# Seven half-block products for gate and up in the last group of a ternary gated FFN

## The chip, the cores and the metric

One core of a Trainium2 chip runs one program. The time is the device time of a run in microseconds. A core has TensorE (PE, matrix products into PSUM), VectorE (DVE), ScalarE (ACT), GpSimd (POOL) and SyncE (SP, which here issues nearly all DMAs). Each engine works through its own instructions in order; semaphores tie them together. PSUM has eight banks of 128 x 512 single-precision numbers.

## The reference

Input x is 2 x 1024 x 512 in single precision. Cut to what matters:

```
x = x + gated_delta(layernorm(x), Wq, Wk, Wv, Wo, Wb, bb, Wd, bd)   # a linear attention with a scan over time
n = layernorm(x)                          # [2, 1024, 512]
quantize(w) = clip(round(w / (mean|w| + 1e-8)), -1, 1)
gate = n @ quantize(w1).T                 # w1, w2: [1408, 512]
up   = n @ quantize(w2).T
x = x + (sigmoid(gate) * up) @ quantize(w3).T       # w3: [512, 1408]
```

The weights become -1, 0 and 1, which half precision holds exactly. An activation is split into a high half-precision part and the rest, a low one; both are multiplied, and PSUM adds them.

## The kernel before, in words

The 1024 time steps are 8 chunks of 128 for each of the 2 batch rows. Attention goes chunk by chunk. The FFN goes by groups of two chunks (`G = 4` groups, 512 tokens each). While group g is in the FFN, the attention and second normalisation of chunks 2g+2 and 2g+3 are worked in between its units; group 3 has no such work.

A group has `UNITS = 15` units (`group`, L1186 on TensorE). Units 0 to 10 are the 11 blocks of 128 hidden rows: 8 matmuls of 512 columns for gate, 8 for up (4 blocks of the contraction, high and low part, L1199), into three PSUM banks in turn (`bank_free`, L1174). ScalarE takes the sigmoid of gate (L718) and then the high part of the hidden block (L724), VectorE multiplies up with the sigmoid (L989, one operand in PSUM) and subtracts for the low part (L994). Units 11 to 14 are the down products of the four token blocks, 22 matmuls each (L1217); the last of the whole kernel is made in two halves of 256 columns. VectorE adds each to the residual (L1005) and SP stores it.

The order is written out by hand. Tables `PE_AFTER`, `DVE_AFTER`, `ACT_AFTER`, `POOL_AFTER` (L238 on) say behind which unit of group g the steps of the two next chunks stand on each engine: `chain`, `levels`, `masks`, `o`, `state`, `oT`, `wo`, `resid`, `norm2`, `apply`, `xhi`, `xlo`. The last ones prepare the next group's tokens. `norm2` gives mean and variance (VectorE) and the scale (six small GpSimd instructions, L402 to L408); `apply` (L915) writes the normalised, scaled values; `xhi` (L651, ScalarE) makes the high part, `xlo` the low one, for batch row 0 on GpSimd (L480) and for row 1 on VectorE (L921). SP then issues two DMA transposes of 128 x 1024 (L319, `turn_x`), which lay the tokens along the free dimension. For the second chunk these stand at units 11 and 12, beside the down products. TensorE waits for all transposes of a group at its start:

```
pe.wait_ge(xT_in, 64 * g + 64)
```

PSUM holds three banks `ffn` for the FFN; `lev`, `oc` (two banks each) and `pd` are the attention's, unused in group 3.

Of the kernel before, what the change touches and what calls it, by code (L numbers as in the profile page):

```python
# [16 lines left out]
def build_gated_delta_ternary_ffn(nc, x, Wq, Wk, Wv, Wo, Wb, bb, Wd, bd, w1, w2, w3, out):  # L17
# [5 lines left out]
    P = 128  # L23
# [11 lines left out]
    XS = 2048.0  # L35
# [3 lines left out]
    assert B == 2 and 2 * K == P and V == P and DT == 4 and XS * D ** 0.5 < 65504 and HS * D < 65504  # L39
# [7 lines left out]
    with ctx:  # L47
# [14 lines left out]
        wqk = sb("wqk", [P, DT, 2 * K])  # L62
        wbd = sb("wbd", [P, DT, 2 * K])
        wv = sb("wv", [P, DT, V])
# [7 lines left out]
        xn = sb("xn", [P, 2, B, D])  # L72
        xn2 = sb("xn2", [P, B, D])
# [28 lines left out]
        xT = w_nat[:, WN:WN + G * XT].bitcast(f16).rearrange("p (g s t n) -> p g s t n", g=G, s=2, t=DT)  # L102
        abs_out = [w12T[:, DT * k:DT * k + DT, 2 * P:2 * P + SL // DT] for k in range(2)]
        late = xnT[:, :, :, :, :].rearrange("p a t b n -> p (a t b n)")
        sig = late[:, 0:2 * 512].rearrange("p (s n) -> p s n", s=2)
        hid32 = late[:, 2 * 512:4 * 512].rearrange("p (s n) -> p s n", s=2)
# [9 lines left out]
        xT_last = w_nat[:, WN + (G - 1) * XT:WN + G * XT]  # L116
        scratch_front = [Scratch(w3T_flat[:, 8 * P * n:8 * P * (n + 1)]) for n in range(2)]
        scratch_late = [Scratch(xT_last[:, 8 * P * n:8 * P * (n + 1)]) for n in range(2)]
# [44 lines left out]
                                                    sem("lo_ready"))  # L163
        down_done, y_ready, y_stored = sem("down_done"), sem("y_ready"), sem("y_stored")
# [77 lines left out]
        POOL_AFTER = {"fetch": (0, 3), "norm2": (6, 11), "xlo": (7, 12)}  # L242

# [16 lines left out]

        def xT_tile(c, b):

            at = 2 * (c % 2) + b
            return xT[:, c // 2, :, :, at * P:(at + 1) * P].rearrange("p s t n -> p (s t) n")
# [14 lines left out]
        def _(sp_):  # L279
# [35 lines left out]
            def turn_x(c):  # L315

                for b in range(B):
# [37 lines left out]
            for g in range(G):  # L355
                for u in range(UNITS):
# [5 lines left out]
                    if g < G - 1:  # L362
                        for s, k in stages(DVE_AFTER, u):
                            if s == "xlo":
                                turn_x(2 * g + 2 + k)
# [5 lines left out]
        def _(pool):  # L371
# [92 lines left out]
            def norm2(c):  # L464
                pool.wait_ge(stats2_ready, c + 1)
                rstd(c, C + c, mv2, rs2, XS).then_inc(rstd2_ready, 1)

            def attn(s, c):
                if s == "fetch":
                    fetch(c)  # L470
                if s == "norm2":
                    norm2(c)
                if s == "xlo":
                    xlo(c)

            def xlo(c):
                if c > 1:
                    pool.wait_ge(xT_in, 16 * B * (c - 1))
                pool.wait_ge(xhi_ready, B * c + 1)
                nc.gpsimd.tensor_tensor(halves(c)[:, 0, 1, :], xn2[:, 0, :], halves(c)[:, 0, 0, :],  # L480
                                        ALU.subtract).then_inc(xlo0_ready, 1)

# [17 lines left out]
            for u in range(UNITS):  # L500
                for s, k in stages(POOL_AFTER, u):
                    if (s, k) != ("fetch", 0):
                        attn(s, 2 + k)
# [7 lines left out]
            for g in range(1, G - 1):  # L511
# [5 lines left out]
                norm2(2 * g + 2)  # L517
                xlo(2 * g + 2)
                norm2(2 * g + 3)
                xlo(2 * g + 3)  # L520
                if g == 1:
                    gates(7)

        @block.scalar
        def _(act):
# [105 lines left out]
            def attn(s, c):  # L631
# [624 lines left out]
```

## Time and profile before

| | us |
|---|---|
| runs, median (lowest to highest) | 328.49 (328.21 to 328.55) |
| profiled execution, first to last instruction (span) | 327.1 |
| TensorE busy | 319.8 (98%) |
| VectorE busy | 210.1 (64%) |
| ScalarE busy | 142.4 (44%) |
| GpSimd busy | 107.4 (33%) |
| L1199, gate and up: 704 matmuls | 155.4 |
| L1217, down: 374 matmuls | 76.7 |

The page gives the profiled execution's span and no other time of it; the runs' times are taken around the program and hold a little more. Busy is the time in which an engine had at least one instruction under way. A matmul's own duration (379 ns for 512 columns) is longer than the distance to the next, since they are pipelined; sums are made with the distance. "Idle before, releaser" names what ended the idle time in front of an instruction.

### The profile page before, as it was taken

Reading aid. Unit: us, or ns where it says so; the run is one execution under the profiler, and the core shown is the slowest. Engines: PE = TensorE matmul, PEld = TensorE weight load, DVE = VectorE, ACT = ScalarE, POOL = GpSimd, SP = SyncE. Lnnn points to the kernel's source line nnn. Section 1 sums busy time; section 2 is a strip of 40 time slices with the busy share of each in tenths; the row PEclk is TensorE's granted clock in tenths of the full one; section 3 lists DMA queues with packets and bytes.
Section 4 is the critical chain, followed back from the end, with each engine's and each line's share of the span. In section 5 each row is a group of like instructions: output and inputs, shape, how many; then the busy total and the mean of one; then the engine's idle time right before and its main releaser. Section 6 shows DMA issues by size and latency. Waiting matters only on the chain.

```text
span 327.1 us, 5876 instructions
## 1 busy us (share of the span) xinstructions
PE 319.8 (98%) x2152; PEld 176.1 (54%) x2152; DVE 210.1 (64%) x474; ACT 142.4 (44%) x281; POOL 107.4 (33%) x339
## 2 busy tenths in 40 slices
PE   7999999999999999999999999999999999999996
PEld 5888779874445444445454444454544444444445
DVE  6789899899998767366688543666886312433311
ACT  3687896789855571323143260231431102232200
POOL 7298325599913016980030136500201100000000
PEclk9999999999999999999999999999999999999999
DMA  6999900647841625300003051000030720000011
GB/s 180 382 388 395 360 4 0 104 91 133 125 85 32 114 49 81 113 0 2 0 2 64 2 129 61 7 2 0 2 64 0 93 102 1 0 2 0 0 66 64
DMA packets 45805, 26.99 MB, mean 83 GB/s; under 512 B 37584, under 2 KB 38352, under 8 KB 45776
## 3 DMA queue, kind: packets, MB, share of 16 engines
q1 hardware_dynamic: 45456, 26.62, 31.0%
q8 instruction: 17, 0.28, 0.4%
q14 instruction: 12, 0.10, 0.1%
q10 hardware_dynamic: 320, 0.00, 0.0%
HBM read 13.89 MB, written 4.19 MB: 55 GB/s over the span
## 4 chain that ended last, share of the span: by engine, by line
PE 78%; DVE 10%; DMA 3%; SPq 3%; ACT 2%; issue 2%; DVEq 0%; ACTq 0%
PE ffn L1199 40%; PE ffn L1217 23%; PE lev L1120 4%; DMA x_sb<-in_L_attn_x_dram 3%; PE ffn L1044 3%; DVE w_nat L841 2%; DVE X L854 2%; SPq L282 2%; PE lev L1077 2%; PE pd L1054 2%; PE oc L1104 1%; DVE abs_part L821 1%; DVE w_nat L848 1%; DVE xnT L989 1%; DVE sc L881 1%
## 5 line engine op out<-in xcount | busy, mean ns | idle before, releaser
L1199 PE MATMUL ffn<-w_nat,w12T 128*128 128x512 f16 x704 | 155.4, 379 | 0.6 <-DVE xnT L989 0.6
L1199 PEld LDWEIGHTS ffn<-w_nat,w12T 128*128 128x128 f16 x704 | 67.8, 98 | 83.0 <-issue 3.7
L1217 PE MATMUL ffn<-w3T,w_nat 128*128 128x512 f16 (+1 forms) x374 | 76.7, 366 | 0.0
L718 ACT ACTIVATE xnT<-ffn 128x512 f32<-128x512 f32 x44 | 26.1, 593 | 97.5 <-PE ffn L1199 97.5
L989 DVE SCALAR_TENSOR_TENSOR xnT<-ffn,xnT 128x512 f32<-128x512 f32 x44 | 30.2, 687 | 52.3 <-PE ffn L1199 51.9
L1217 PEld LDWEIGHTS ffn<-w3T,w_nat 128*128 128x128 f16 x374 | 36.6, 98 | 40.7 <-ACT w_nat L724 1.0
L402 POOL TENSOR_TENSOR ve<-mv,rconst 128x2 f32<-128x2 f32 x12 | 2.5, 210 | 118.1 <-DVE mv L758 118.1
L1005 DVE SCALAR_TENSOR_TENSOR x_sb<-ffn,x_sb 128x512 f32<-128x512 f32 (+1 forms) x17 | 11.2, 659 | 42.8 <-PE ffn L1217 42.8
L994 DVE TENSOR_TENSOR w_nat<-xnT,w_nat 128x512 f16<-128x512 f32 x44 | 32.2, 732 | 0.4
L724 ACT ACTIVATE w_nat<-xnT 128x512 f16<-128x512 f32 x44 | 27.4, 623 | 8.4 <-DVE xnT L989 8.3
L881 DVE COPY_PREDICATED sc<-mask,lev 128x128 f32<-128x128 uint32 x56 | 18.9, 338 | 2.9 <-PE oc L1091 1.3
L854 DVE TENSOR_TENSOR X<-X,tmk 128x256 f32<-128x256 f32 x42 | 19.1, 454 | 1.4
L754 DVE BATCH_NORM_STATS2 stats<-x_sb 128x6 f32<-128x512 f32 x26 | 16.7, 683 | 0.4
L1044 PE MATMUL ffn<-xnT,wqk 128*128 128x256 f32 x64 | 15.7, 389 | 1.2 <-ACT xnT L542 0.8
L1054 PE MATMUL pd<-wv,xnT 128*128 128x128 f32 x128 | 15.8, 275 | 0.0
L1054 PEld LDWEIGHTS pd<-wv,xnT 128*128 128x128 f32 x128 | 15.2, 192 | 0.6 <-issue 0.5
L613 ACT ACTIVATE q<-w_nat,unround 128x512 f16<-128x512 f32 x22 | 14.3, 711 | 2.4 <-DVE w_nat L841 1.6
L1044 PE MATMUL ffn<-xnT,wbd 128*128 128x256 f32 x64 | 15.1, 379 | 0.0
L1120 PE MATMUL lev<-wo,oT 128*128 128x512 f32 x28 | 13.3, 598 | 0.6 <-DVE S L896 0.5
L1044 PEld LDWEIGHTS ffn<-xnT,wqk 128*128 128x128 f32 x64 | 11.5, 190 | 3.4 <-issue 1.0
L1044 PEld LDWEIGHTS ffn<-xnT,wbd 128*128 128x128 f32 x64 | 12.2, 190 | 1.7
L440 POOL TENSOR_TENSOR tot<-tot 128x32 f32<-128x32 f32 (+5 forms) x48 | 12.4, 258 | 0.0
(142 smaller groups left out, 368.2 us busy)
## 6 DMA issues: line engine op xcount, KB each, us to landing
x_sb<-in_L_attn_x_dram SPq DMA_DIRECT2D x16, 256.0 KB, 8.4
out_dram<-x_sb SPq DMA_DIRECT2D x15, 256.0 KB, 2.0
w_nat<-in_L_ffn_w_dram SPq DMA_DIRECT2D x2, 1536.0 KB, 12.2
w_nat<-in_L_ffn_w_dram SPq DMA_DIRECT2D x2, 1408.0 KB, 14.7
w_nat<-in_L_ffn_w_dram SPq DMA_DIRECT2D x2, 1280.0 KB, 12.9
wv<-in_L_attn_Wv_dram SPq DMA_DIRECT2D x1, 256.0 KB, 5.8
wo<-in_L_attn_Wo_dram SPq DMA_DIRECT2D x1, 256.0 KB, 13.5
out_dram<-x_sb SPq DMA_DIRECT2D x2, 128.0 KB, 1.7
```

The source lines that it names most:

```text
L718: nc.scalar.activation(sig[:, u % 2, :], bank[2 * u % 3][:, :], ACT.Sigmoid, scale=1.0 / XS).then_inc(sig_ready, 1)
L724: nc.scalar.activation(hid[:, 0, u - 1, :], hid32[:, (u - 1) % 2, :], ACT.Copy).then_inc(hi_ready, 1)
L754: done = nc.vector.bn_stats(stats[:, c, b, :], tile(c, b))
L854: step = nc.vector.tensor_tensor(FG(c, l + 1).rearrange("p (n h) -> p n h", h=h), FG(c, l).rearrange("p (n h) -> p n h", h=h), factors(c, ...
L881: link(nc.vector.copy_predicated(sc[:, :, :].rearrange("p b (n two h) -> p b n two h", two=2, h=h)[:, :, :, 1, :], level(mask[:, l, :], l) ...
L989: nc.vector.scalar_tensor_tensor(hid32[:, u % 2, :], bank[(2 * u + 1) % 3][:, :], HS / XS, sig[:, u % 2, :], ALU.mult, ALU.mult).then_inc( ...
L994: nc.vector.tensor_tensor(hid[:, 1, u - 1, :], hid32[:, (u - 1) % 2, :], hid[:, 0, u - 1, :], ALU.subtract).then_inc(lo_ready, 1)
L1044: done = nc.tensor.matmul(z_bank(c)[:, a * 256:(a + 1) * 256], w[:, t, :], turned(c)[:, t, :, :], start=t == 0, stop=t == DT - 1)
L1054: done = nc.tensor.matmul(pd[:, b * V:(b + 1) * V], turned(c)[:, t, b, :], wv[:, t, :], start=t == 0, stop=t == DT - 1)
L1120: done = nc.tensor.matmul(wo_bank(c, b)[:, :], oT[:, b, :], wo[:, :], start=True, stop=True)
L1199: done = nc.tensor.matmul(bank[n % 3][:, :], w12T[:, a * DT + t, u * P:(u + 1) * P], xT[:, g, part, t, :], start=t == 0 and part == 0, sto ...
L1217: done = nc.tensor.matmul(bank[(2 * HT + m + h) % 3][:, cols], hid[:, part, j, m * P:(m + 1) * P], w3T[:, j, cols], start=part == 0 and j ...
```

## The change

Group 3 (`FAST`) computes gate and up differently; groups 0 to 2 keep their products. The normalised tokens of group 3 are seen as a 2 x 2 block matrix: A11, A12 are the first and second 256 features of batch row 0 (`xn2(0)`), A21, A22 those of row 1. The weights are a 2 x 2 block matrix too, gate and up, each with its first and second 256 features. The product of two 2 x 2 block matrices takes eight block products; here it takes seven, of sums of blocks, which are added up in shared sums (products 1 to 7 below). Each block product of a unit is 128 hidden rows by 256 tokens with a contraction of 256.

- Weight sums `T1` to `T4` (128 x 2 x 1408 in half precision) are made on VectorE in group 2, behind units 2, 3, 4 and 11 (`T_AT`); T1 overwrites a block of up that is no longer needed.
- Token sums `xsum` (four, 128 x 256 each) are made on GpSimd for chunks 6 and 7. The plain blocks (3 of 256) and the sums (4 of 256) are split in high and low parts and turned by two DMA transposes a chunk, of 1536 and 2048 columns. The scale of the tokens is 512 in place of 2048.
- Four banks serve: unit u has a bank for products 1, 6, 7, 4 (`bank_a`) and one for 2, then 5, 3 (`bank_c`). ScalarE copies product 1 into `bank_c` as the seed on which product 2 adds, and keeps copies of the sums after product 6 and 7; VectorE adds them to `bank_c` for up; the multiplication with the sigmoid moves from VectorE to GpSimd, in two halves.
- Units k and k-1 are interleaved on TensorE. Product 1 of unit 0 stands four matmuls before the end of group 2. The last unit's products 4 and 3 stand among the first down matmuls.
- Moved: for chunk 7 SP's transposes stand at unit 13 in place of 12, behind the store of the second down tile, and `xlo` on VectorE at 13. The sums' splits: high on ScalarE at units 8 and 13, low on GpSimd.
- Tables for a group that follows another fast one are in the code too; with `FAST = (3,)` they are not used. `w_proj`, `x_all`, `xT(g)` and `scratch_late` lay memory out anew.

The products, in the order of one unit; the code writes A21, A22 as `A11(1)`, `A12(1)`:

| product | bank | weights | tokens | TensorE waits for |
|---|---|---|---|---|
| 1 | a | gate_w[0] | A11 | sigmoid_b of unit u-2 |
| 6 | a | T2 | A21 + A22 - A11 | seed |
| 2 | c (on the seed) | gate_w[1] | A12 | nothing more |
| 7 | a | T3 | A11 - A21 | keep_u2 |
| 5 | c | T1 | A21 + A22 | sigmoid_a |
| 4 | a | T4 | A22 | keep_u3 |
| 3 | c | up_w[1] | A12 - (A21 + A22 - A11) | up_b |

```diff
-    XS = 2048.0
+    XS, XS_FAST = 2048.0, 512.0
+    FAST = (3,)
+    HP = 2 * P
...
+        T1 = w12T[:, DT:DT + 2, :]
+        gate_w = [w12T[:, 2 * n:2 * n + 2, :] for n in range(2)]
+        up_w = [w12T[:, DT + 2 * n:DT + 2 * n + 2, :] for n in range(2)]
...
+        DVE_NEXT_FAST = DVE_AFTER | {"xlo": (8, 13)}
+        ACT_NEXT_FAST = {"gt": (2, 7), "oT": (4, 9), "xhiN": (7, 12), "xhiS": (8, 13)}
+        SP_NEXT_FAST = {"turn": (9, 13)}
...
+        T_AT = {2: (3,), 3: (2,), 4: (4,), HT: (1,)}
...
+        def bank_a(u):
+            return (bank[2], pd)[u % 2]
+        def bank_c(u):
+            return bank[u % 2]
...
+                if is_fast(c):            # SP, turn_x
+                    sp_.wait_ge(xlo1_ready, c + 1)
+                    sp_.dma_start_transpose(xT_N..., flat_N[c % 2]).then_inc(xT_in, 16)
+                    sp_.wait_ge(xlo0_ready, c + 1)
+                    sp_.dma_start_transpose(xT_S..., flat_S[c % 2]).then_inc(xT_in, 16)
...
+                if is_fast(c):            # GpSimd, xlo
+                    pool.wait_ge(xhi_ready, B * c + 2)
+                    for n in range(4):
+                        done = nc.gpsimd.tensor_tensor(split_S[c % 2][:, n, 1, :], xsum[:, n, :],
+                                                       split_S[c % 2][:, n, 0, :], ALU.subtract)
+                    done.then_inc(xlo0_ready, 1)
...
+                nc.gpsimd.tensor_tensor(xsum[:, 2, :], A11(0), A11(1), ALU.subtract)      # sums0
+                link(nc.gpsimd.tensor_tensor(xsum[:, 0, :], A11(1), A12(1), ALU.add))
+                link(nc.gpsimd.tensor_tensor(xsum[:, 1, :], xsum[:, 0, :], A11(0), ALU.subtract))   # sums1
+                nc.gpsimd.tensor_tensor(xsum[:, 3, :], A12(0), xsum[:, 1, :], ALU.subtract).then_inc(sums_ready, 1)
...
+            for g in FAST:                # GpSimd
+                for k in range(HT + 2):
+                    if k > 1:
+                        hidden_a(g, k - 2)
+                    if 1 <= k <= HT:
+                        hidden_b(g, k - 1)
...
+            def fast_group(g):            # ScalarE
+                for k in range(HT + 1):
+                    if k > 0:
+                        keep_u3(g, k - 1)
+                    if k < HT:
+                        seed(g, k)
+                    if k > 1:
+                        hidden_hi(g, k - 2)
+                    if k < HT:
+                        keep_u2(g, k)
+                    if k > 0:
+                        sigmoid_b(g, k - 1)
+                    if k < HT:
+                        sigmoid_a(g, k)
+                hidden_hi(g, HT - 1)
...
+                if n == 3:                # VectorE, weight_sum
+                    done = nc.vector.tensor_tensor(T3, up_w[1], up_w[0], ALU.subtract)
+                if n == 2:
+                    done = nc.vector.tensor_tensor(T2, T3, gate_w[0], ALU.add)
+                if n == 4:
+                    done = nc.vector.tensor_tensor(T4, gate_w[1], T2, ALU.subtract)
+                if n == 1:
+                    done = nc.vector.tensor_tensor(T1, up_w[0], gate_w[0], ALU.subtract)
...
+            def fast_group(g):            # VectorE
+                for k in range(HT + 1):
+                    if k > 0:
+                        up_b(g, k - 1)
+                    if k > 1:
+                        hidden_lo(g, k - 2)
+                    if k > 0:
+                        up_a(g, k - 1)
+                hidden_lo(g, HT - 1)
...
+                            if m == DT - 1 and n == 2 * HT - 4 and g + 1 in FAST:   # TensorE, group 2
+                                pe.wait_ge(xT_in, 64 * g + 128)
+                                product1(g + 1, 0)
...
+            def product(out, weights, u, tokens, first):
+                for t in range(2):
+                    for part in range(2):
+                        done = nc.tensor.matmul(out[:, 0:HP], weights[:, t, u * P:(u + 1) * P], tokens[:, part, t, :],
+                                                start=first and t == 0 and part == 0, stop=t == 1 and part == 1, skip_group_check=not first)
+                return done
...
+            def fast_group(g):            # TensorE
+                pe.wait_ge(T_ready, 4)
+                for k in range(HT):
+                    if k > 0:
+                        product1(g, k)
+                        product5(g, k - 1)
+                        product4(g, k - 1)
+                    product6(g, k)
+                    product2(g, k)
+                    if k > 0:
+                        product3(g, k - 1)
+                    product7(g, k)
+                pe.wait_ge(sig_b_ready, fast_n(g, HT - 1))
+                pe.wait_ge(hi_ready, g * HT + 6)
+                product5(g, HT - 1)
+                for n in range(2):
+                    down(g, 0, n, LATE_LAST)
+                product4(g, HT - 1)
+                for n in range(2, 6):
+                    down(g, 0, n, LATE_LAST)
+                product3(g, HT - 1)
+                for n in range(6, 2 * HT):
+                    part, j = LATE_LAST[n]
+                    pe.wait_ge((hi_ready, lo_ready)[part], g * HT + j + 1)
+                    down(g, 0, n, LATE_LAST)
...
```

## Rows read from the trace of the kernel before

**Rows 1.** The page, busy time of the engines and the granted clock in 40 slices
```profile
PE 319.8 (98%) x2152; PEld 176.1 (54%) x2152; DVE 210.1 (64%) x474; ACT 142.4 (44%) x281; POOL 107.4 (33%) x339
...
PEclk9999999999999999999999999999999999999999
```

**Rows 2.** Window of gate and up in group 3: length, busy us by engine, granted clock, DMA share
```profile
267.40:305.40 38.00, 38.00 (x178) 17.21 (x176) 12.98 (x20) 11.75 (x21) 0.00 (x0) 1.00 0.02 8
```

**Rows 3.** The chain that ended last, its last pieces: start, us, what
```profile
267.44 37.99 PE ffn L1199 x176
305.43 19.06 PE ffn L1217 x110
```

**Rows 4.** Timeline, end of the last down tile: start, us, engine, line, op [idle before <-releaser]
```profile
322.11 0.42 DVE L1005 SCALAR_TENSOR_TENSOR x_sb<-ffn,x_sb 128x256 f32<-128x256 f32 x1 [1.71 <-PE ffn L1217]
324.51 0.42 DVE L1005 SCALAR_TENSOR_TENSOR x_sb<-ffn,x_sb 128x256 f32<-128x256 f32 x1 [1.98 <-PE ffn L1217]
324.20 0.27 PE L1217 MATMUL ffn<-w3T,w_nat 128*128 128x256 f16 x1
```

**Rows 5.** Groups by line and shape from 190 us: count, then busy us and mean ns of one
```profile
L1199 PEld LDWEIGHTS ffn<-w_nat,w12T 128*128 128x128 f16 x352 | 34.1, 98 | 41.4 <-issue 0.9
...
L724 ACT ACTIVATE w_nat<-xnT 128x512 f16<-128x512 f32 x22 | 13.7, 623 | 4.2 <-DVE xnT L989 4.2
L718 ACT ACTIVATE xnT<-ffn 128x512 f32<-128x512 f32 x22 | 13.1, 597 | 67.9 <-PE ffn L1199 67.9
...
L480 POOL TENSOR_TENSOR xn<-xn 128x512 f16<-128x512 f32 x2 | 2.3, 1152 | 2.9 <-ACT xn L651 2.9
...
L639 ACT ACTIVATE oT<-oc 128x256 f32<-128x256 f32 x2 | 0.8, 384 | 2.1 <-PE lev L1109 1.8 <-PE oc L1104 0.3
...
L424 POOL TENSOR_TENSOR w_nat<-w_nat 128x128 f32<-128x128 f32 x1 | 0.5, 456 | 6.2 <-DVE w_nat L813 6.2
```

**Rows 6.** Timeline in group 0, a matmul that waited for VectorE
```profile
89.18 0.67 DVE L989 SCALAR_TENSOR_TENSOR xnT<-ffn,xnT 128x512 f32<-128x512 f32 x1
...
90.00 1.24 PE L1199 MATMUL ffn<-w_nat,w12T 128*128 128x512 f16 x5 [0.55 <-DVE xnT L989]
```

**Rows 7.** Timeline of VectorE, units 2 to 5 of group 2
```profile
217.38 0.69 DVE L989 SCALAR_TENSOR_TENSOR xnT<-ffn,xnT 128x512 f32<-128x512 f32 x1 [0.47 <-PE ffn L1199]
...
220.84 0.69 DVE L989 SCALAR_TENSOR_TENSOR xnT<-ffn,xnT 128x512 f32<-128x512 f32 x1 [2.17 <-PE ffn L1199]
...
225.58 0.69 DVE L989 SCALAR_TENSOR_TENSOR xnT<-ffn,xnT 128x512 f32<-128x512 f32 x1 [2.84 <-PE ffn L1199]
```

**Rows 8.** Timeline, chunk 7 from its statistics to its transposes
```profile
253.23 0.69 DVE L1005 SCALAR_TENSOR_TENSOR x_sb<-ffn,x_sb 128x512 f32<-128x512 f32 x1 [1.58 <-PE ffn L1217]
...
253.60 0.20 POOL L408 TENSOR_TENSOR rs<-rs 128x2 f32<-128x2 f32 x1
253.84 0.99 DVE L915 TENSOR_SCALAR xn<-x_sb,mv,rs 128x512 f32<-128x512 f32 x2
...
254.47 1.15 ACT L651 ACTIVATE xn<-xn 128x512 f16<-128x512 f32 x2 [6.35 <-DVE xn L915]
255.24 1.15 POOL L480 TENSOR_TENSOR xn<-xn 128x512 f16<-128x512 f32 x1 [1.45 <-ACT xn L651]
255.72 1.22 DVE L921 TENSOR_TENSOR xn<-xn 128x512 f16<-128x512 f32 x1 [0.89 <-ACT xn L651]
256.42 2.62 SPq L319 DMA_TRANSPOSE w_nat<-xn  x2
257.98 0.69 DVE L1005 SCALAR_TENSOR_TENSOR x_sb<-ffn,x_sb 128x512 f32<-128x512 f32 x1 [1.04 <-PE ffn L1217]
```

**Rows 9.** DMA issues in 237 to 238 and in 256 to 257 us: count, median us to landing
```profile
w_nat<-xs SPq DMA_TRANSPOSE x1, 3.0
...
w_nat<-xn SPq DMA_TRANSPOSE x1, 5.0
```

**Rows 10.** Timeline of VectorE, the low halves of chunk 6
```profile
240.94 0.68 DVE L921 TENSOR_TENSOR xs<-xn,xs 128x512 f16<-128x512 f32 x1
```

More of the change, by code:

```diff
@@ L510, in _ @@
             gates(4)
-            for g in range(1, G - 1):
+            for g in range(1, FAST[0]):
                 fetch(2 * g + 2)
@@ L739, in _ @@
             for g in range(G):
-                group(g)
+                if g in FAST:
+                    fast_group(g)
+                else:
+                    group(g)
         @block.vector
@@ L871, in attn @@
                     chain(c, range(4, NL))
-                if s == "masks":
+                if s == "chainA":
+                    dve.wait_ge(factors_ready, c + 1)
+                    dve.wait_ge(stored, c + 1)
+                    dve.wait_ge(o_done, c)
+                    chain(c, (0,))
+                if s == "chainB":
+                    chain(c, (1, 2))
+                if s == "chainC":
+                    chain(c, (3,))
+                if s == "chainD":
+                    chain(c, (4, 5))
+                if s == "chainE":
+                    chain(c, (6,))
+                if s == "norm2a":
+                    dve.wait_ge(resid_ready, c + 1)
+                    carry_wait()
+                    nc.vector.bn_stats(stats2[:, c, 0, :], tile(c, 0))
+                if s == "norm2b":
+                    link(nc.vector.bn_stats(stats2[:, c, 1, :], tile(c, 1)))
+                    carry_wait()
+                    for b in range(B):
+                        done = nc.vector.bn_aggr(mv2[:, c, b, :], stats2[:, c, b, :])
+                    done.then_inc(stats2_ready, 1)
+                if s == "sums":
+                    dve.wait_ge(xn2_ready, B * c + 2)
+                    dve.wait_ge(xhi_ready, B * c)
+                    nc.vector.tensor_tensor(xsum[:, 2, :], A11(0), A11(1), ALU.subtract)
+                    link(nc.vector.tensor_tensor(xsum[:, 0, :], A11(1), A12(1), ALU.add))
+                    link(nc.vector.tensor_tensor(xsum[:, 1, :], xsum[:, 0, :], A11(0), ALU.subtract))
+                    nc.vector.tensor_tensor(xsum[:, 3, :], A12(0), xsum[:, 1, :], ALU.subtract).then_inc(sums_ready, 1)
+                if s == "xloS":
+                    dve.wait_ge(xhi_ready, B * c + 2)
+                    nc.vector.tensor_tensor(split_S[c % 2][:, :, 1, :], xsum[:, :, :], split_S[c % 2][:, :, 0, :],
+                                            ALU.subtract).then_inc(xlo0_ready, 1)
+                if s in ("masks", "masks0", "masks1", "masks2", "masks3"):
                     dve.wait_ge(levels_done, c + 1)
@@ L1222, in group @@
-                    if g < G - 1:
-                        for s, k in stages(PE_AFTER, u):
-                            attn(s, 2 * g + 2 + k)
+                        for n in range(2 * HT):
+                            if m == 0:
+                                pe.wait_ge((hi_ready, lo_ready)[n // HT], g * HT + n % HT + 1)
+                                if g == 0 and n < HT:
+                                    pe.wait_ge(w3_in[n % QS], 16 * (n // QS + 1))
+                            if m == DT - 1 and n == 2 * HT - 4 and g + 1 in FAST:
+                                pe.wait_ge(xT_in, 64 * g + 128)
+                                product1(g + 1, 0)
+                            down(g, m, n, PARTS_IN_TURN)
@@ L1225, in group, with down @@
+                    for s, c in PE_AT.get((g, u), ()):
+                        attn(s, c)
                     if g == 0 and u == 0:
                         spread(1)
+            PARTS_IN_TURN = [(part, j) for part in range(2) for j in range(HT)]
+            LATE_LAST = ([(part, j) for part in range(2) for j in range(HT - 3)]
+                         + [(part, j) for j in range(HT - 3, HT) for part in range(2)])
+            def down(g, m, n, order):
+                part, j = order[n]
+                done = nc.tensor.matmul(down_bank(g, m)[:, :], hid_at(g, part, j, m), w3T[:, j, :], start=n == 0,
+                                        stop=n == 2 * HT - 1)
+                if n == 2 * HT - 1:
+                    done.then_inc(down_done, 1)
@@ new lines, in down_last @@
+            def down_last(g, m):
+                for h in range(2):
+                    cols = slice(h * D // 2, (h + 1) * D // 2)
+                    for n, (part, j) in enumerate(PARTS_IN_TURN):
+                        done = nc.tensor.matmul(down_bank(g, m + h)[:, cols], hid_at(g, part, j, m), w3T[:, j, cols],
+                                                start=n == 0, stop=n == 2 * HT - 1)
+                    done.then_inc(down_done, 1)
+            def product(out, weights, u, tokens, first):
[4 more added lines that the diff above has]
+                return done
```

376 lines of the change are left out of this document (309 added, 67 removed).

## The prediction

> **What bounds the kernel now.** I read the page's first parts, then the windows by stage, then the chain of waits, then single instructions. TensorE is busy 319.8 of 327.1 us, and the granted clock of full speed, 2.4 GHz, holds throughout [rows 1]. In the stretch that the change rewrites it is busy 38.00 of 38.00 us, while VectorE has 12.98, ScalarE 11.75 and GpSimd nothing to do [rows 2]. The chain that ended last is, from 267.44 to the last addition, TensorE alone: 37.99 us of gate and up in 176 matmuls of 512 columns, then 19.06 us of down [rows 3]. So what is taken out of TensorE's group 3 comes out of the span, if nothing new is late. 37.99/176 is 215.9 ns each. The page gives the span, 327.1 us; the median of the runs is 328.49, so 1.4 us lie around it. The change doesn't touch them (the last store is the same), so I move the median by what the span changes.
>
> **Part 1, the products.** Before: 11 units x 2 x 8 matmuls of 512 columns. After: 11 units x 7 products x 4 matmuls (two blocks of the contraction, high and low part) of 256 columns, 308. What a 256-column matmul with its own weight load costs is shown by the last down tile, which is 2 x 22 of them: the VectorE additions behind its halves start at 322.11 and 324.51 [rows 4], so 22 take 2.40 us, 109.1 ns each. Weight loads of 98 ns [rows 5] stay hidden with 11 ns to spare. 308 x 109.1 ns = 33.60. Gain: 37.99 - 33.60 = **4.4 us**. A unit shrinks from 3.45 to 3.05 us; a product is 0.436. Down keeps its 66 matmuls of 512 and 44 of 256 columns.
>
> **Part 2, the way through ScalarE and back.** Three partial sums of a unit are copied out before TensorE adds to them: seed (after product 1, for 6), u2 (after 6, before 7), u3 (after 7, before 4 in the next turn). In the order 1(k) 5(k-1) 4(k-1) 6(k) 2(k) 3(k-1) 7(k) two products stand between each pair, 0.873 us. The way: a matmul of 256 columns shows 0.27 us [rows 4] where the next follows after 0.109, so 0.16 to its end; 0.04 to the next engine (the last one runs from 324.20, the addition starts at 324.51 [rows 4]); a 128x256 copy out of PSUM 0.384 [rows 5]; back to TensorE 0.15 (VectorE's 0.67 us from 89.18 end at 89.85, the matmul that waited starts at 90.00 [rows 6]). Sum 0.73: no stall, 0.14 to spare. ScalarE's work in a unit is 5 x 0.384 + 0.62 = 2.54 of 3.05 us, VectorE's 2 x 0.42 + 0.68 [rows 4, 10] = 1.53. GpSimd gets two multiplications of 128x256, of which there is no row: 128x128 takes 0.456, 128x512 1.152 [rows 5]. The line between them gives 0.69; the ends are 0.58 (half the larger) and 0.91 (twice the smaller). I take 0.69, which lies between rows of the same operation: 1.4 a unit.
> At the start less stands between: product 7 of unit 0 comes one product after 6, so 0.73 - 0.44 = 0.3 us of stall. At the end, product 5 of unit 10 comes a product sooner after its sigmoid than in a steady turn: 0 to 0.3. Behind the last product 3 stand 0.20, then 0.42 (VectorE), 0.15, 0.69 (GpSimd), 0.10, 0.62 (ScalarE), 0.03, 0.68 (VectorE) and 0.15 back, 3.0 us, against 15 down matmuls of 0.216 put ahead of the one that needs it, 3.24: no stall. Group 3 loses 0.3 + half of 0.3, rounded to **0.5 us**; ends 0.3 and 1.5 (each of the three ways 0.17 longer than I take is 0.03 over the room, 0.9 in 10 turns, beside 0.3 and 0.3). Before, a bank came back to TensorE after a unit of 3.45 us; this cover of 0.14 us is what is left of it.
>
> **Part 3, hidden work in group 2.** VectorE gets four weight sums of 128 x 2816 half-precision numbers. No row has all operands in half precision. By elements, from the 0.42 us of an operation on 256 [rows 4] and the 0.68 of one on 512 [rows 10], 1.0 ns each, one is 0.68 + 2304 x 1.0 ns = 2.98; by bytes, half of the operands' width, some 1.55. I take 1.55, since inputs and output are all half as wide; 2.98 is the other end. Three of them stand behind units 2 to 4 of group 2, where VectorE waited 0.47, 2.17 and 2.84 us for TensorE [rows 7]: 4.65 against 5.48 of idle, and a filled bank has 3.45 us until TensorE wants it back. Cost 0. At 2.98 they need 8.9, and the state update of chunk 6 slips some 0.9 behind TensorE's wo product. The fourth is in part 4.
> The Trainium skill (VectorE: DVE Perf Modes, What auto-detection actually checks) says that a two-source operation whose tensors are all 16 bits wide passes two elements a cycle; no run here shows it yet. By it these sums stay hidden; by one element a cycle the result would be 2.3 us worse.
>
> **Part 4, the tokens' transposes, which become late.** Today, for chunk 7: its factors done on GpSimd at 253.80, normalising 253.84 to 254.83, high halves from 254.47, low halves to 256.94, transposes issued from 256.42 [rows 8], the first landed 5.0 us later [rows 9]; TensorE wants them at 267.44 [rows 3]. The new chain:
> - T1 stands behind the first down addition, which starts at 253.23 and frees VectorE 0.62 later: 253.85 to 255.4. Then normalising, 1.0: 256.4, where it was 254.83.
> - Four sums of halves on GpSimd, the last three each needing the one before or standing behind it: 0.15 (the wait shown from ScalarE's 255.09 to 255.24) + 0.62 + 0.78 + 0.78 + 0.69 = 3.0: 259.4.
> - Their high halves, one ScalarE instruction of 1024 elements: 0.62 + 512 x 0.83 ns (the slope between 256 and 512 in rows 5) = 1.05, with 0.1 of wait: 260.6.
> - Their low halves, four GpSimd instructions: 0.15 + 3 x 0.62 + 0.69 = 2.7: 263.3.
> - The transpose of 2048 columns. Two of 1024 hold the queue for 2.62 us [rows 8], and one that nothing disturbed landed 3.0 us from issue [rows 9], so 1.7 behind the end of its 1.3. Now 2.6 + 1.7 = 4.3: 267.6.
> TensorE asks earlier than before, as product 1 of unit 0 stands four down matmuls before the end of group 2: 267.44 - 0.86 = 266.6. Stall, with 0.1 to restart: 267.7 - 266.6 = **1.1 us**, paid also by the four down matmuls and all that is queued behind. The other transpose (1536 columns) needs only ScalarE's first copy and VectorE; it is issued near 260.4, ahead of the late one. SP's store of the second down tile now stands ahead of both, and waits for an addition that is done at 258.67 [rows 8], before 260.4. Ends of the stall: 0 (GpSimd at 0.58 in all eight instructions takes 0.9 off, 0.2 of error the rest) and 4.5 (T1 by elements adds 1.4, a landing after 5.0 in place of 3.0 adds 2.0).
> Chunk 6 has the same additions at units 6 to 8, some 20 us before anything asks for its halves (the normalising of chunk 7, TensorE in group 3). Cost 0. The wait of product 1 of unit 1 for the last down addition is over 0.20 + 0.69 + 0.15 = 1.0 us after the last down matmul, and three products stand between, 1.3 us: cost 0.
>
> **Sum.** -4.4 + 0.5 + 1.1 = -2.8 us: 328.49 - 2.8 = **325.7**.
>
> **A resource that speaks against it.** VectorE's low-half subtraction of 512 columns takes 0.68 us alone, and 1.22 when it starts at 255.72 while GpSimd works from 255.24 to 256.39 [rows 8, 10]. In group 3 GpSimd idled; now it works 1.4 of each 3.05 us, beside one such subtraction a unit. This is rival C. The Trainium skill (GPSIMD Engine Reference, Key points) says that GpSimd shares its SBUF interfaces with VectorE's instructions that have two SBUF inputs. By that rule the trace agrees; the two updates of up in each unit, with one input in PSUM, would be spared.
>
> **Rivals.**
> - A: the transposes are in time and only the stalls at the ends of the loop are paid. 328.49 - 4.4 + 0.4 = 324.5. For it: landed 261.4 against 267.44, six us of room today. Against: ten steps more on three engines. Chance 0.20.
> - B: the landing is as slow as the one shown at this very place. 325.7 + 2.0 = 327.7; with T1 by elements too 329.1. For it: the 5.0 is the one of this place [rows 9]. Against: undisturbed ones 3.0. Chance 0.18.
> - C, the slower one: the ring hidden_hi(k-2), hidden_lo(k-2), up_a(k-1), hidden_a(k-1), hidden_hi(k-1) becomes the bound of a turn, since VectorE's order puts up_a behind hidden_lo. At my values 0.62 + 0.03 + 0.61 + 0.42 + 0.15 + 0.69 + 0.10 = 2.62, under 3.05. With the subtraction at 1.22 and GpSimd at 0.91, 3.45: 0.4 x 10 turns = 4.0 us, 329.7. It stalls from 3.05 on, and the kernel is slower from 3.05 + 2.8/10 = 3.33 on. For it: the 1.22. Against: by the order above hidden_a ends 0.6 us before the subtraction starts and hidden_b begins 0.4 after it. Chance 0.15.
> - The forecast, 325.0 to 326.8: 0.47.
>
> **The numbers.** What a measurement of this kernel can tell from no change is about 0.2%, 0.66 us, so "same" is 327.8 to 329.15. Faster: 0.47 + 0.20 + 0.10 of B = 0.77. Same: 0.06 of B, 0.05 of C = 0.11. Slower: 0.02 of B, 0.10 of C = 0.12. The range leaves out the lower tail of A and the upper parts of B and C: 324.2 to 328.7.
>
> **What would show it.** Part 1: starts 109 ns apart, the loop at 33.6 us and its stalls. Part 2: TensorE idle behind a ScalarE copy once, 0.3 us; the same release in each unit shows the way or ring C. Part 3: four VectorE rows of some 1.55 us. Part 4: TensorE idle about 1 us before the first product 1, released by a DMA; GpSimd's sums near 0.69. The prediction is wrong if that idle time is missing (A) or over 2.5 us (B), or if a steady turn is longer than 3.1 us (C).

## The result and the profile after

| | before | after |
|---|---|---|
| median of 15 runs, us | 328.54 | 327.70 |
| lowest to highest, us | 328.21 to 329.14 | 326.35 to 328.54 |
| ratio after / before | | 0.9965 (0.9953 to 0.9977) |
| span of the profiled execution, us | 327.1 | 324.7 |
| its whole run, us | | 326.43 |

The kernel is faster by 0.35%, 1.1 us by the ratio, where 2.8 us were forecast. The runs fall into two bands. Seven of the 15 have a mean granted clock of 0.999 to 1.000 and take 326.35 to 327.16 us (median 326.64), eight have 0.995 and take 327.70 to 328.54 (median 328.15). The profiled execution is of the lower band. So there are two errors to find: 0.9 us in the lower band (1.9 us gained in place of 2.8), and 1.5 us that about half of the executions pay on top.

The page of the changed kernel, with span, busy times and granted clock, to be set against [rows 1]:

```profile
span 324.7 us, 6312 instructions
...
PE 315.7 (97%) x2284; PEld 189.0 (58%) x2284; DVE 219.5 (68%) x489; ACT 157.0 (48%) x325; POOL 134.5 (41%) x375
...
PEclk9999999999999999999999999999999999999999
```

The chain that ended last, from T1 to the first product (start, us, what), to be set against [rows 3, 8]:

```profile
253.37 1.60 DVE w12T L1294
...
255.00 1.01 DVE x_all L1213 x2
...
258.38 1.33 POOL x_all L626
...
259.73 1.06 ACT x_all L825
...
260.93 2.57 POOL x_all L606 x4
...
263.52 4.60 DMA w_nat<-x_all
...
268.16 0.61 PE ffn L1615 x4
```

Each step that the forecast named for chunk 7 is on it, in its order. Beside it, in the timeline, stand VectorE's subtraction of the plain blocks, GpSimd's fourth sum and the other transpose:

```profile
258.10 1.02 DVE L1218 TENSOR_TENSOR w_proj<-x_all,w_proj 128x768 f16<-128x768 f32 x1
...
258.38 1.32 POOL L626 TENSOR_TENSOR x_all<-x_all 128x256 f32<-128x256 f32 x1
259.14 1.55 SPq L433 DMA_TRANSPOSE w_nat<-w_proj  x1
```

The fourth sum takes 1.32 us where the other three take 0.73, and the subtraction 1.02: the two ran side by side. What TensorE did then (timeline, with idle time and releaser in brackets), and the first return from ScalarE:

```profile
268.16 0.61 PE L1615 MATMUL ffn<-w_nat,w12T 128*128 128x256 f16 x4 [2.08 <-DMA w_nat<-x_all]
...
270.54 0.33 PEld L1615 LDWEIGHTS ffn<-w_nat 128*128 128x128 f16 x4 [0.32 <-ACT w_nat L939]
```

The view counts idle time from the modelled end of the matmul before. From start to start it is a little more: the 19 down matmuls from 261.82 on would put the next start at 265.92, and it comes at 268.16, 2.24 us late.

One steady turn, with GpSimd's two multiplications L635 (second half) and L643 (first half), ScalarE's high part L974 and VectorE's low part L1365:

```profile
286.04 0.42 DVE L1359 SCALAR_TENSOR_TENSOR q<-ffn,w_nat 128x256 f32<-128x256 f32 x1 [0.24 <-PE ffn L1615]
...
289.10 0.42 DVE L1359 SCALAR_TENSOR_TENSOR q<-ffn,w_nat 128x256 f32<-128x256 f32 x1 [0.24 <-PE ffn L1615]
289.11 0.73 POOL L635 TENSOR_TENSOR xnT<-xnT,q 128x256 f32<-128x256 f32 x1 [1.64 <-ACT xnT L966]
...
289.80 0.73 POOL L643 TENSOR_TENSOR xnT<-xnT,q 128x256 f32<-128x256 f32 x1
...
290.56 0.63 ACT L974 ACTIVATE w_nat<-xnT 128x512 f16<-128x512 f32 x1 [0.22 <-POOL xnT L643]
...
291.22 0.69 DVE L1365 TENSOR_TENSOR w_nat<-xnT,w_nat 128x512 f16<-128x512 f32 x1 [0.39 <-ACT w_nat L974]
```

From one update of up to the next (L1359, 286.04 and 289.10) it is 3.06 us. GpSimd ends at 290.53 and the subtraction runs from 291.22: they don't meet. The groups by line and shape (count, busy us and mean ns of one) say the same for all units, and price the weight sums; the last two pieces of the chain, 22 matmuls each, compare with [rows 4]:

```profile
L635 POOL TENSOR_TENSOR xnT<-xnT,q 128x256 f32<-128x256 f32 x11 | 8.0, 730 | 26.6 <-ACT xnT L966 25.1 <-DVE w_nat L1365 1.5
...
L1365 DVE TENSOR_TENSOR w_nat<-xnT,w_nat 128x512 f16<-128x512 f32 x11 | 7.6, 692 | 5.9 <-ACT w_nat L974 5.9
...
L1294 DVE TENSOR_TENSOR w12T<-w12T 128x2816 f16<-128x2816 f16 x1 | 1.6, 1618 | 0.0
```

```profile
317.28 2.40 PE pd L1607 x22
319.68 2.42 PE ffn L1607 x22
```

### The profile page after: what moved, and what is told of

Same layout as the page of the kernel before. It is cut to its first block, busy times and chain, and to the rows that moved or that the text cites. A ratio compares the mean times of both kernels' runs of the same rounds, so it can differ in the third digit from the quotient of the medians.

```text
span 324.7 us, 6312 instructions
## 1 busy us (share of the span) xinstructions
PE 315.7 (97%) x2284; PEld 189.0 (58%) x2284; DVE 219.5 (68%) x489; ACT 157.0 (48%) x325; POOL 134.5 (41%) x375
## 4 chain that ended last, share of the span: by engine, by line
PE 77%; DVE 11%; ACT 4%; issue 3%; POOL 3%; DMA 1%; DVEq 0%; POOLq 0%; ACTq 0%
PE ffn L1568 29%; PE ffn L1597 15%; PE ffn L1615 8%; PE ffn L1413 6%; PE lev L1489 3%; PE pd L1615 3%; DVE w_nat L1102 2%; PE pd L1423 2%; DVE X L1115 2%; PE lev L1500 2%; PE lev L1446 2%; PE pd L1597 1%; DMA w_nat<-x_all 1%; PE ffn L1401 1%; PE oc L1473 1%
## 5 line engine op out<-in xcount | busy, mean ns | idle before, releaser
L1568 PE MATMUL ffn<-w_nat,w12T 128*128 128x512 f16 x528 | 117.2, 379 | 0.5 <-DVE xnT L1315 0.4
L1597 PE MATMUL ffn<-w3T,w_nat 128*128 128x512 f16 x308 | 67.3, 379 | 0.0
L1315 DVE SCALAR_TENSOR_TENSOR xnT<-ffn,xnT 128x512 f32<-128x512 f32 x33 | 22.6, 685 | 21.8 <-PE ffn L1568 21.4
L1413 PE MATMUL ffn<-xnT,w_proj 128*128 128x256 f32 x128 | 29.5, 384 | 1.2 <-ACT xnT L718 0.8
L1413 PEld LDWEIGHTS ffn<-xnT,w_proj 128*128 128x128 f32 x128 | 23.7, 190 | 5.1 <-issue 1.0
L1320 DVE TENSOR_TENSOR w_nat<-xnT,w_nat 128x512 f16<-128x512 f32 x33 | 25.0, 757 | 0.3
L1615 PE MATMUL ffn<-w_nat,w12T 128*128 128x256 f16 x156 | 21.0, 273 | 2.1 <-DMA w_nat<-x_all 2.1
L635 POOL TENSOR_TENSOR xnT<-xnT,q 128x256 f32<-128x256 f32 x11 | 8.0, 730 | 26.6 <-ACT xnT L966 25.1
L1423 PE MATMUL pd<-w_proj,xnT 128*128 128x128 f32 x128 | 15.8, 275 | 0.0
L1423 PEld LDWEIGHTS pd<-w_proj,xnT 128*128 128x128 f32 x128 | 15.2, 192 | 0.6 <-issue 0.5
L1489 PE MATMUL lev<-wo,oT 128*128 128x512 f32 x28 | 13.3, 598 | 0.6 <-DVE S L1193 0.5
```

What stands on the lines that cost most here:

```text
L1315: nc.vector.scalar_tensor_tensor(hid32[:, u % 2, :], bank[(2 * u + 1) % 3][:, :], HS / XS, sig[:, u % 2, :], ALU.mult, ALU.mult).then_inc( ...
L1320: nc.vector.tensor_tensor(hid[:, 1, u - 1, :], hid32[:, (u - 1) % 2, :], hid[:, 0, u - 1, :], ALU.subtract).then_inc(lo_ready, 1)
L1413: done = nc.tensor.matmul(z_bank(c)[:, a * 256:(a + 1) * 256], w[:, t, :], turned(c)[:, t, :, :], start=t == 0, stop=t == DT - 1)
L1423: done = nc.tensor.matmul(pd[:, b * V:(b + 1) * V], turned(c)[:, t, b, :], wv[:, t, :], start=t == 0, stop=t == DT - 1)
L1489: done = nc.tensor.matmul(wo_bank(c, b)[:, :], oT[:, b, :], wo[:, :], start=True, stop=True)
L1568: done = nc.tensor.matmul(bank[n % 3][:, :], w12T[:, a * DT + t, u * P:(u + 1) * P], xT(g)[:, part, t, :], start=t == 0 and part == 0, sto ...
```

## The experiments

All ratios are against the kernel before on the same chip. "Clock" is the mean granted clock of a run.

**e1_again: the changed kernel, no edit.**

> The changed kernel once more, unchanged. Theory K (the clock): TensorE's idle time of 2.08 us before product 1 of unit 0 lets the granted clock fall to its lower level for some microseconds in about half of the executions. Then the runs again fall into two bands, mean clock 1.000 at 326.3 to 327.2 us and mean clock 0.995 at 327.7 to 328.5 us, and the clock is low in a stretch right behind that idle time. Rival L (the transfer): the upper band is a landing that is 1.5 to 2 us later, and the clock's 0.005 is something else; then a slow execution shows an idle time of 3.5 us or more in the same place.

12 runs: median 327.09 us, ratio 0.9966 (0.9949 to 0.9983). Seven have a clock of 0.999 or more, 326.49 to 327.21 us; five have 0.995, 328.00 to 329.01. This time the profiled execution is one of the five, so the lost time can be seen. Its windows around the start of group 3 (PEclk is the granted clock, 0.50 the lower of its two levels, 1.2 GHz):

```profile
core 0: us, PE busy (x) PEld busy (x) DVE busy (x) ACT busy (x) POOL busy (x), PEclk, DMA share, GB/s
268.00:269.20 1.20, 0.94 (x7) 0.66 (x8) 0.00 (x0) 0.29 (x1) 0.00 (x0) 1.00 0.05 17
269.20:272.60 3.40, 3.40 (x16) 2.05 (x15) 0.69 (x1) 0.84 (x3) 0.00 (x0) 0.50 0.21 77
272.60:276.00 3.40, 3.40 (x33) 3.00 (x32) 0.85 (x2) 1.87 (x6) 0.61 (x1) 0.99 0.01 2
```

and its chain:

```profile
263.61 4.61 DMA w_nat<-x_all
...
268.26 0.61 PE ffn L1615 x4
268.87 1.24 PE ffn L1597 x4
270.11 2.56 PE ffn L1615 x12
```

The transpose landed after 4.61 us as in the other band, so rival L is wrong. TensorE starts again at 268.26, and from 269.2 to 272.6, 3.4 us, it is granted half the clock; in those it does 1.7 us of work at the full one. The pieces show it: four matmuls of 512 columns behind product 1 take 1.24 us (0.86 before), and 12 of 256 take 2.56 (1.31). The span, 326.3, is 1.6 us over the other band's 324.7.

**e2_t1_late: T1 out of the chain.**

```diff
-        T_AT = {2: (3,), 3: (2,), 4: (4,), HT: (1,)}
+        T_AT = {2: (3,), 3: (2,), 4: (4,), HT + 2: (1,)}
```

> One edit to the changed kernel: the weight sum T1 stands behind unit 13 of group 2 instead of 11, so that it no longer delays chunk 7's normalising. The chain to the last transpose moves up by T1's 1.62 us: idle time before product 1 from 2.08 to about 0.5 us. By the sum of my prediction the profiled span goes from 324.7 to 323.1. Theory K adds that with 0.5 us of idle time the clock holds and the upper band is gone: all runs 324.6 to 325.2, mean clock 1.000. Rival L: two bands stay, both 1.6 lower, 324.8 and 326.5. If something else holds the transposes (SP's order, the other transpose) the idle time stays at 2.08 and nothing changes.

6 runs: 324.93 us (324.44 to 325.74), ratio 0.9896 (0.9876 to 0.9915), clock 1.000 in all. From the timeline:

```profile
253.59 1.00 DVE L1213 TENSOR_SCALAR x_all<-x_sb,mv,rs 128x512 f32<-128x512 f32 x2
...
256.96 0.72 POOL L626 TENSOR_TENSOR x_all<-x_all 128x256 f32<-128x256 f32 x1
...
258.34 0.95 DVE L1218 TENSOR_TENSOR w_proj<-x_all,w_proj 128x768 f16<-128x768 f32 x1
...
261.73 1.34 SPq L436 DMA_TRANSPOSE w_nat<-x_all  x1
...
263.09 1.62 DVE L1294 TENSOR_TENSOR w12T<-w12T 128x2816 f16<-128x2816 f16 x1
...
266.29 0.33 PEld L1615 LDWEIGHTS ffn<-w_nat,w12T 128*128 128x128 f16 x4 [0.46 <-DMA w_nat<-x_all]
```

Normalising starts at once, and T1 runs late in the shadow. A second thing went with it: the fourth sum has 0.72 us again, since VectorE's subtraction now comes after it. The last row is product 1's first weight load: it waited 0.46 us for the DMA, where the changed kernel's waited 2.57. So this run takes out T1's 1.62 us and the 0.6 us of the slowed sum together.

**e3_filled: the idle time filled, the transposes as late as ever.**

```diff
+                                pe.wait_ge(resid_ready, C)
+                                keep_warm(16)
                                 pe.wait_ge(xT_in, 64 * g + 128)
```

> One edit to the changed kernel: 16 matmuls of 256 columns into a bank that nobody reads stand ahead of the wait for the transposes (16 x 0.109 = 1.75 us of the 2.08 us idle time). The transposes land as late as before, so the work is as late; only TensorE isn't idle. Theory K: mean clock 1.000 in all runs, all in the lower band, 326.3 to 327.0. Rival L: two bands as in the changed kernel, median near 327.7. If the filling is longer than the idle time of an execution it costs at most 0.2 us.

6 runs: 326.88 us (326.86 to 327.41), ratio 0.9953 (0.9938 to 0.9969), clock 0.999 to 1.000 in all. TensorE's timeline:

```profile
266.35 1.91 PE L1500 MATMUL lev<-ident 128*128 128x256 f16 x16
268.60 0.61 PE L1617 MATMUL ffn<-w_nat,w12T 128*128 128x256 f16 x4 [0.34 <-DMA w_nat<-x_all]
```

The work is no earlier, product 1 starts at 268.60, and the upper band is gone. The unedited kernel had a low clock in 13 of 27 runs, and at that rate six clean ones in a row would come by chance 2 times in 100. That the idle time, and not the lateness, brings the clock down is shown by this run together with the next.

**e4_before_idle: the kernel before with TensorE held.**

```diff
+            pool.wait_ge(down_done, 11)                      # GpSimd, at its end
+            for n in range(7):
+                link(nc.gpsimd.tensor_tensor(X[:, 0, :], X[:, 1, :], X[:, 2, :], ALU.add))
+            nc.gpsimd.tensor_tensor(X[:, 3, 0:P], X[:, 1, 0:P], X[:, 2, 0:P], ALU.add).then_inc(held, 1)
...
+                                    if (g, m, part, j) == (2, DT - 1, 1, HT - 4):      # TensorE
+                                        pe.wait_ge(held, 1)
```

> The kernel before, with no part of the change, but with TensorE held at the same place (ahead of the last four down matmuls of group 2) until eight otherwise idle GpSimd additions are done, 2.1 us after it gets there. Theory K: two bands here too, about 330.6 with mean clock 1.000 and 332.2 with 0.995. Rival L, and a second rival (M: the seven-product loop itself, with twice as many matmuls and weight loads and four engines busy, lets the clock fall): one band only, at 330.6, clock 1.000.

6 runs: 331.44 us, ratio 1.0099 (1.0077 to 1.0121). Four have a clock of 0.999 or more (330.99 to 331.48 us), two 0.995 (332.70, 332.71): two bands, 1.4 us apart, with none of the seven-product code in the kernel. Rival M is wrong as the cause, and L again. The idle time was 2.31 us:

```profile
269.05 1.04 PE L1224 MATMUL ffn<-w3T,w_nat 128*128 128x512 f16 x4 [2.31 <-POOL X L527]
```

**e10_idle_15: the same with seven additions in place of eight** (`range(6)`).

> The kernel before with TensorE held at the same place as in e4_before_idle, by seven GpSimd additions in place of eight: idle time 2.3 - 0.8 = 1.5 us, 329.9 us where the clock holds, 1.6 more where it falls. Theory K expects fewer or no executions with mean clock 0.995 than the 2 of 6 at 2.3 us; the same share of them in both would say that the length of the idle time doesn't matter down to 1.5 us.

5 runs: 330.24 us (329.90 to 331.12), ratio 1.0059 (1.0046 to 1.0073), clock 1.000 in all.

```profile
267.82 1.04 PE L1224 MATMUL ffn<-w3T,w_nat 128*128 128x512 f16 x4 [1.53 <-POOL X L527]
```

**e9_apart: GpSimd's sums and VectorE's subtraction one after the other.**

```diff
                     dve.wait_ge(xhi_ready, B * c + 1)
+                    dve.wait_ge(sums_ready, c - 2 * FAST[0] + 1)
                     nc.vector.tensor_tensor(split_N[c % 2][:, :, 1, :],
```

> One edit to the changed kernel: VectorE's low-half subtraction of the plain blocks waits until GpSimd's four token sums are done, so that the two don't run side by side. If the fourth sum took 1.32 us in place of 0.73 because of that subtraction, it takes 0.73 now and the last transpose lands 0.6 us earlier: idle time 2.08 to 1.5 us, lower band 326.0. If the 1.32 us has another cause, nothing moves. Theory K leaves open whether 1.5 us of idle time is still enough for the clock to fall; if it isn't, the upper band goes.

5 runs: 326.21 us (325.65 to 326.78), ratio 0.9928 (0.9914 to 0.9941), clock 1.000 in all. The fourth sum on GpSimd's timeline, and TensorE's wait for the transposes (us in total, times, longest):

```profile
259.32 0.73 POOL L626 TENSOR_TENSOR x_all<-x_all 128x256 f32<-128x256 f32 x1
...
PE ffn L1616 <- DMA w_nat<-x_all: 1.5, 1, 1.5
```

That the two run side by side is the cause of the 1.32: with a wait added to keep them apart, the kernel is faster, by 0.6 us of idle time and by the upper band. Over the two kernels whose profiled execution has 1.5 us of idle time, 0 of 10 runs had a low clock; over those with 2.1 to 2.3 us, 15 of 33 (8 of 15, 5 of 12, 2 of 6). In the runs that were not profiled, the idle time is taken from the profiled one and the fall of the clock from the mean. The two kernels with 1.5 us ran on another chip than e1 to e4, so this count compares lengths across chips; e1, e2, e3 and e4 ran on one chip. The kernel before shows 0.999 or 1.000 in all of its 35 runs that list a clock.

**e8_sums_only and e5_sums_dve: chunk 7's token sums on VectorE**, with T1 left behind unit 11 (e8) or behind unit 13 (e5).

```diff
-        DVE_NEXT_FAST = DVE_AFTER | {"xlo": (8, 13)}
+        DVE_NEXT_FAST = DVE_AFTER | {"sums": (None, 12), "xlo": (8, 13)}
...
-                    if is_fast(c):
+                    if is_fast(c) and c % 2 == 0:
```

> The second of these edits alone: T1 stays behind unit 11, the sums of chunk 7 go to VectorE. The chain is 1.1 to 1.7 us shorter (the second figure if GpSimd's last sum, 1.32 us beside VectorE's subtraction, was slowed by it), so the idle time goes from 2.08 to 0.4 to 1.0 us and the profiled span to 323.0 to 323.6. Theory K: if that is too short for the clock to fall, one band near 325.1; rival L: two bands, the upper 1.6 us higher.

> Two edits to the changed kernel: T1 behind unit 13, and the four token sums of chunk 7 on VectorE (four linked operations of 128x256, 4 x 0.43 + waits = about 1.8 us) in place of GpSimd (0.73 each and 2.9 us in all with the waits). The last transpose lands 1.1 us earlier than with T1 moved alone, where 0.2 to 0.3 us of idle time were left. Theory K and the sum: no idle time before product 1, clock 1.000 in all runs, about 324.7 us, so most of the 4.4 us of part 1 is there. If a further loss hides in the seven-product loop, the gain against the kernel before stays under 3.5 us though the idle time is gone.

e8, 4 runs: 325.25 us, ratio 0.9895 (0.9882 to 0.9909), clock 1.000 in all. e5, 4 runs: 324.70 us (324.57 to 325.10), ratio 0.9876 (0.9861 to 0.9891), clock 0.999 or 1.000, no idle time before product 1. The chain of e8 has the four sums at 1.7 us, where GpSimd took 3.6 (256.09 to 259.71) in the changed kernel:

```profile
256.06 0.43 DVE x_all L1159
...
257.32 0.44 DVE x_all L1162
...
261.64 4.63 DMA w_nat<-x_all
```

Both times came out as expected; two lengths did not. In e8 the chain is 1.9 us shorter (last transpose issued at 261.64 in place of 263.52), with 1.7 expected at most. In e5 the last transpose was to land 1.1 us earlier than in e2, and from the start of the first down addition it lands after 13.0 us (253.29 to 266.27) for 13.3 in e2 (252.98 to 266.25): 0.3 us earlier. The shorter chain met VectorE's subtraction in another place:

```profile
257.84 3.26 POOL L606 TENSOR_TENSOR x_all<-x_all 128x256 f16<-128x256 f32 x4 [3.98 <-ACT x_all L825]
...
258.64 1.31 DVE L1218 TENSOR_TENSOR w_proj<-x_all,w_proj 128x768 f16<-128x768 f32 x1
```

GpSimd's four low halves took 3.26 us (2.56 in the changed kernel), and the landing 4.8 for 4.5. TensorE, which no longer waits there, paid nothing for it. e5 has the lowest median and beats both kernels: 1.24%, 4.1 us by the ratio, close to part 1 (4.4) less the 0.2 of the first return. Between e2 and e5 the medians differ by 0.2 us, within their spread; e2 is the smaller edit.

**e6_fast23 and e7_fast23_early: group 2 by seven products too**, alone and with the two edits of e5.

```diff
-    FAST = (3,)
+    FAST = (2, 3)
```

> One edit to the changed kernel: FAST = (2, 3), so that group 2 goes by seven products too, with the attention of chunks 6 and 7 in between. Its matmuls take 4.4 us less again. If the stall in front of the first fast group is all that was missed, it stands now in front of group 2, and a second one in front of group 3 with the longer list of steps: 320.5 to 324. If the cover of 0.14 us on the way through ScalarE isn't enough once VectorE, ScalarE and GpSimd also work for the attention, group 2 shows idle time in many units and the time stays at 324 to 328.

> The same with T1 behind unit 13 of group 1 and the sums of chunk 5 on VectorE: the idle time in front of group 2 goes, 2 us less than the kernel with FAST = (2, 3) alone, in both of the cases named there.

e6, 4 runs: 331.53 us, ratio 1.0078 (1.0059 to 1.0097). e7, 5 runs: 331.99 us, ratio 1.0094 (1.0080 to 1.0108), clock 0.984 to 0.990. Both misses. Who TensorE waited for in e6 (us in total, times, longest), and two windows of 10 us:

```profile
PE ffn L1615 <- DMA w_nat<-x_all: 3.9, 2, 2.2
PE lev L1446 <- DVE X L1115: 3.7, 2, 3.0
...
PE lev L1446 <- DVE x_sb L1200: 0.8, 1, 0.8
...
200.00:210.00 10.00, 5.28 (x91) 3.24 (x90) 7.04 (x15) 1.32 (x4) 7.84 (x36) 0.96 0.41 103
210.00:220.00 10.00, 10.00 (x84) 7.68 (x83) 5.83 (x16) 5.83 (x15) 3.88 (x12) 0.87 0.02 4
```

My expectation named the cover in ScalarE's way as the danger; TensorE waited for none of it. It waited 3.0 us for VectorE's level chain of chunk 6, 0.8 for a residual, and twice for transposes (1.7 and 2.2), and the clock fell behind the long wait: it is granted half from 209.2 to 212.6, 3.4 us. From product 1 of group 2 (202.97) to that of group 3 (271.96) it takes 69.0 us, where the kernel before needs 65.4 (from 0.86 ahead of its group 2, which starts at 202.07, to 266.58): 65.4 - 4.4 + 3.0 + 0.8 + 2.2 (the second wait for a transpose) + 1.7 for the clock (10 us at 0.96 and 10 at 0.87) = 68.7.

In e7 product 1 of group 2 starts 1.9 us sooner, at 201.11. But T1, moved behind unit 13 of group 1, now runs in the middle of that level chain on VectorE, and TensorE goes on with the levels no sooner than in e6 (207.46):

```profile
203.96 1.58 DVE L1294 TENSOR_TENSOR w12T<-w12T 128x2816 f16<-128x2816 f16 x1
...
207.38 0.44 PE L1446 MATMUL lev<-store 64*64 64x32 f32 x8 [4.80 <-DVE X L1115]
```

The wait grew from 3.0 to 4.8 us and took back what was won. The clock fell within it and stayed at half for 6.8 us (205.1 to 211.9), and once more for 3.4 us (273.3 to 276.7) behind the 2.1 us wait for group 3's transposes, where in e6 2.2 us at the same place left it at 1.00. The second stretch costs 1.7 of the 2.0 us by which the spans (330.5 and 328.5) differ.

## Why the prediction was wrong

- **Part 1, right.** The seven-product loop runs at the 109 ns taken from the last down tile. A turn takes 3.06 us, forecast 3.05. The gain of 4.4 us is there, as e5 shows with 4.1 net of the other costs.
- **Part 2, right in kind, too dear.** 0.5 us was put down for returns; the loop shows one stall, 0.2 us at product 7 of unit 0 (the product starts at 270.55, two products after 269.47 would be 270.34). The end of the loop cost nothing. GpSimd's 128x256 took 0.73 for my 0.69 of [rows 5]; the copy 0.38 as in [rows 5]. (VectorE's 2 x 0.42 + 0.68 is 1.52, not 1.53.)
- **Part 3, right.** The four weight sums take 1.62 us each for 1.55. So the choice by bytes, not by elements (2.98), holds. By the rule of the Trainium skill cited there (VectorE: DVE Perf Modes, What auto-detection actually checks) the trace agrees, with 1.62 us for each sum.
- **Part 4, the step that failed: the mechanism was right, its price was not, and what the idle time does to the clock was missing.** "Stall, with 0.1 to restart: 267.7 - 266.6 = 1.1 us" measured 2.08, by the same view. Everything in front of the stretch was 0.5 us earlier in this execution than in the one before, so I compare lengths. From the start of the first down addition (252.74 now) to the normalised values (256.01) it is 3.3 us, forecast 3.2. The four sums, with the wait in front of them, took 3.7 us (to 259.71) for 3.0, and 0.6 of that is the slowing that the prediction's own paragraph on a resource describes, in a place where I had not looked for it; I had put VectorE's subtraction into the chain of the other transpose ("needs only ScalarE's first copy and VectorE") and didn't lay it beside GpSimd's sums. e9 takes exactly this out. The landing took 4.60 for 4.3, the rest is 0.1. One more term was left out: 267.44 in [rows 3] is where the matmul before ends, while the first gate matmul starts 0.16 sooner, at 267.28. A stall thus loses 0.16 us more than its idle time (2.24 here; in e10 1.53 us of idle time cost 1.7 between the medians).
- **The clock.** The forecast reads "paid also by the four down matmuls and all that is queued behind": idle time at its own length. In 15 of 33 runs of the three kernels with 2.1 to 2.3 us of it, the mean granted clock was 0.995, and where the profile caught it (e1) the clock was at 1.2 GHz for 3.4 us, which cost 1.7 us of work. The profile before could have warned: its clock was at full speed throughout, the idle time before an FFN product in the rows was 0.55 us [rows 6], and the longest that TensorE waited there, once it had begun, was 0.8. I took a price from a kernel without a pause of this length. By lengths the lower band gains 4.4 - 0.2 - 2.2 = 2.0 us (1.9 between the medians), and 1.9 - 1.5 x 8/15 = 1.1, what the ratio says.
- **Rivals.** A was wrong on the changed kernel and came true in e5, 324.70 us for 324.5; its sum takes 0.4 where part 2 has 0.5. B was wrong: the landing took 4.5 to 4.8 us in the seven profiled executions with `FAST = (3,)`, the 4.3 of the forecast and 0.2 to 0.5 more, not 6.3. C was wrong: low parts took 0.691 to 0.693 us in all 11 units, never beside GpSimd. By the rule of the Trainium skill (GPSIMD Engine Reference, Key points), which names VectorE's instructions with two SBUF inputs, the trace agrees in both directions: L626 and L1218, which met, took 1.32 and 1.02 us, apart 0.73 and 0.96, while VectorE's updates with one input in PSUM kept 0.42 beside GpSimd's multiplications.

## What to carry to other kernels

Where a kernel's TensorE hardly pauses, a new wait can cost more than its length: here 1.5 us cost only itself, and 2.1 us cost 1.5 us more in about half of the runs. Ask whether such a wait can be moved or shortened. Filling it with 16 matmuls that nobody reads took the second band away, but it is worth less: the median came out 0.2 us under the unedited kernel's on the same chip, within both intervals. A step that prepares the next stage should hold only what that stage's first instruction needs; T1, needed only after the tokens' first product, stood in front of their preparation; moving it, which also ended the meeting of the fourth sum with the subtraction, gave 1.7 us even against the lower band on the same chip (326.58 to 324.93). Two engines' instructions that are each priced alone must be laid beside each other in time: one of them was slowed by 0.6 us by the other, and adding a wait between them made the kernel faster.

## What the runs showed of the hardware that I had not expected

- 2.1 to 2.3 us without a matmul were followed by a mean granted clock of 0.995 in 15 of 33 runs, 1.5 us in 0 of 10 (on another chip). Where a profile caught the fall, the clock was at its lower level for 3.4 us, from 0.9 to 1.7 us after TensorE had started again (e1, e6 and the second wait of e7); in the 4.8 us wait of e7 it fell before TensorE started again and stayed down for 6.8 us.
- With `FAST = (3,)`, chunk 7's 2048-column transpose landed 4.5 to 4.8 us after issue and the 1536-column one 3.7 to 4.1, against 3.0 for an undisturbed one of 1024 [rows 9]. How long SP's queue is held does not follow the columns. I had scaled 1.3 us for 1024; 2048 columns held it for 1.32 us in the changed kernel's chunk 7, 2.05 in e5's and 2.74 in the changed kernel's chunk 6. The latter two were issued within 1.5 us of the transpose before; why they held it longer is not shown.
- Beside VectorE it is not always GpSimd that keeps its pace. In [rows 8] GpSimd's 1.15 us was the usual one and VectorE was slowed; here GpSimd's sum went from 0.73 to 1.32 us and VectorE's subtraction only from 0.96 to 1.02. In both the one that started later was slowed more (VectorE at 255.72 behind GpSimd at 255.24; GpSimd at 258.38 behind VectorE at 258.10), and so it was in chunk 6, where a sum of 0.73 us took 1.18, started at 236.32 behind a subtraction of VectorE at 236.07. No experiment turned the order round, and in e5 both sides were slowed.
